# Key scaling moved to the head of each slot, own banks for the transposes, and every item of layer 1 by DMA

## The chip, the cores and the metric

One core of a Trainium2 chip runs the whole kernel. A core has five engines that each take their instructions in order: TensorE (PE, with its weight loads as PEld), VectorE (DVE), ScalarE (ACT), GpSimd (POOL) and SyncE (SP, which issues the DMAs here). They meet through semaphores only. The metric is the device time of one execution in microseconds, less is better.

## The reference

The model has two layers. Each adds a gated cross attention and a gated feed-forward to the residual x of 8 batches x 128 tokens x 512. What the change touches is the attention of layer 1 and the passage to its feed-forward:

```
q = (latents @ Wq), 32 heads of 128;  k, v = ([context, latents] @ Wk, Wv), 8 heads of 128
q = rms_norm(q, q_norm_w);  k = rms_norm(k, k_norm_w)
scores = einsum('bhgqd,bhkd->bhgqk', qg, k) * scale
probs  = softmax(scores);  out = einsum('bhgqk,bhkd->bhgqd', probs, v)
x = x + tanh(g_xattn[1]) * (out @ Wo)
x = x + tanh(g_ffn[1]) * (layernorm(x) @ weight.T + bias)
```

## The kernel before

Layer 1 is cut into 64 items: 8 heads of keys and values (the loop index t) times 8 batches (j). An item has 128 queries for each of four query heads and 256 keys, 128 from the context (computed in layer 0, loaded from HBM into kvc) and 128 from the latents. All products are made in three passes on a high and a low part of each operand, so nearly each tile has a "_hi" made by ScalarE and a "_lo" made by VectorE or POOL. What stands in the profile as fbias is, in this stage, k_sb (scaled keys) and k_sq (squares), which lie in that tensor; p is the probabilities, nb the shift of the exponentials, w_hi and w_lo the split weights of the next head.

The stage is a software pipeline written out by hand. Each engine has a function slot1(t, j), unrolled for t = 0 and t = 7 and looped for t = 1 to 6. In slot i (i = 8t+j) the engines work on several items at once, in this order:

- TensorE: keys_values(i+2) into the upper half of bank KVB; transposes of the queries of item i+1 into Q1B, and of its keys into the lower half of KVB; output_projection1(i-2) into Y1B; queries(i+2) into Q1B, which waits until qt_lo(i+1) has been read from there; the scores of item i+1 into S0B and S1B; attention_output1(i-1) into O1B.
- ScalarE: exponentials1(i), which waits for the shift nb; qt_hi and kt_hi of item i+1; pt_hi(i-1), the high part of the transposed probabilities (moved_probabilities_hi); kv_out(i+2), which copies the values and squares the keys of two tiles (the context's and TensorE's); q_out(i+2); output1_hi(i-1).
- VectorE: inverse sums of item i; qt_lo and kt_lo of item i+1; w_lo (split_lo) in slots 1 to 5 of each eight; accumulate1(i-2), drawn as "residual"; probabilities_in_blocks(i), two 32x32 block transposes; v_lo and k_ms of item i+2; w_hi (split_hi) in slots 0 to 4; k_scaled(i+2), which waits for POOL's root k_r; q_ss and q_ms; the maxima nmax and the shift nb of item i+1; output1_lo(i-1), ot_lo.
- POOL: normalises the probabilities of item i in two halves (p, L769); pt_lo(i-1) (L774); the roots k_r and q_r of item i+2 (L631).
- SyncE: the context's keys and values of item i+3; a piece of the next weights; then probabilities_round_trip(i): the blocks go out to DRAM, and four DMAs bring them back transposed.

The probabilities are transposed by that round trip for the first 60 items. For the last four (LAGGED = 60) TensorE transposes them into T0B and T1B, and ScalarE and VectorE split them from there. Behind the last slot stand the rest of the last items and the feed-forward: per batch, row statistics, normalised rows (plain), four transposes, a split, eight matmuls of 512 columns (last_ffn) and the addition to the residual; POOL adds the bias (L653).

## Time and profile before

| | |
|---|---|
| median of 3 runs | 1699.95 us (1699.6 to 1700.13) |
| profiled execution, its own time | 1700.84 us |
| its span | 1699.0 us |
| PE busy | 1651.3 us (97%) |
| DVE busy | 1216.1 us (72%) |
| ACT busy | 987.6 us (58%) |
| POOL busy | 771.7 us (45%) |
| DMA | 216.24 MB, mean 127 GB/s |

Busy time is the time in which an engine had an instruction drawn; a matmul's end is modelled, so PE's share hides small gaps. "<-" in brackets behind a row names what ended the wait in front of it. The span runs from the first to the last instruction; the rest of a run's time lies around it.

### The profile page before, as it was taken

How to read it: one execution, taken by the hardware profiler on the slowest of the kernel's cores; microseconds unless marked ns; L12 is line 12 of the kernel's file. 1: busy time of each engine (PE TensorE's matmuls, PEld its weight loads, DVE VectorE, ACT ScalarE, POOL GpSimd, SP SyncE). 2: the span in 40 equal slices, each digit the busy share in tenths (PEclk: the TensorE clock that was granted, in tenths of full speed). 3: DMA queues.
4: the chain of work that ended last, by engine and by line, in shares of the span. 5: the costliest groups of instructions: out<-in, count | busy, mean ns of one | idle time of the engine just before them, and what ended most of it. 6: DMA issues, size and time to landing. Idle time of an engine off the chain costs nothing.

```text
span 1699.0 us, 30580 instructions
## 1 busy us (share of the span) xinstructions
PE 1651.3 (97%) x9789; PEld 1426.0 (84%) x9789; DVE 1216.1 (72%) x2245; ACT 987.6 (58%) x2480; POOL 771.7 (45%) x644
## 2 busy tenths in 40 slices
PE   9999999999999999999999899999999999999998
PEld 8899999999988888888888777787878787777887
DVE  6444437676787777777788877777777777777777
ACT  5344343345767677676776566565656565665663
POOL 2422223211433443534435565566565656665554
PEclk9999999999999999999999999999999999999999
DMA  6444444545233333333332243434343444433311
GB/s 228 170 173 148 148 166 153 192 138 179 78 104 100 117 108 105 111 100 122 102 112 82 80 141 112 154 117 137 122 151 120 134 136 136 133 123 124 128 57 50
DMA packets 123792, 216.24 MB, mean 127 GB/s; under 512 B 11344, under 2 KB 93648, under 8 KB 120144
## 3 DMA queue, kind: packets, MB, share of 16 engines
q1 hardware_dynamic: 123728, 215.43, 38.0%
q8 instruction: 35, 0.57, 0.1%
q14 instruction: 29, 0.24, 0.0%
HBM read 139.89 MB, written 75.50 MB: 127 GB/s over the span
## 4 chain that ended last, share of the span: by engine, by line
PE 44%; DVE 28%; ACT 12%; issue 10%; POOL 4%; DMA 1%; DVEq 0%; SPq 0%; ACTq 0%; POOLq 0%
PE bank L2163 20%; ACT p L1237 7%; PE bank L2340 6%; DVE probabilities_in_blocks L1983 4%; PE bank L2110 4%; DVE v_lo L1922 3%; PE bank L2112 3%; PE bank L2111 3%; POOL k_r L631 3%; DVE nmax L1954 3%; DVE q_ss L1936 2%; PE bank L2298 2%; PE bank L2376 2%; DVE fbias L1929 2%; DVE qt_lo L2004 2%
## 5 line engine op out<-in xcount | busy, mean ns | idle before, releaser
L712 POOL TENSOR_TENSOR pr<-pr,rn 128x512 f32<-128x512 f32 x64 | 67.5, 1055 | 291.3 <-DVE rn L1610 291.3
L2110 PE MATMUL bank<-w_hi,xt_hi 128*128 (+2 forms) x512 | 182.5, 356 | 11.4 <-DVE qt_lo L2004 6.9
L769 POOL TENSOR_TENSOR p<-p,rn 128x512 f32<-128x512 f32 x128 | 133.2, 1041 | 128.3 <-DVE rn L1964 125.0
L1237 ACT ACTIVATE p<-bank,nb,q_r 128x256 f32<-128x256 f32 x256 | 141.2, 562 | 78.2 <-DVE nb L1959 78.1
L774 POOL TENSOR_TENSOR pt_lo<-probabilities_transposed,pt_hi 128x1024 fp32r<-128x1024 f32 x60 | 168.7, 2811 | 36.2 <-ACT pt_hi L1246 36.2
L2112 PE MATMUL bank<-w_hi,xt_lo 128*128 (+2 forms) x512 | 172.9, 338 | 0.0
L2111 PE MATMUL bank<-w_lo,xt_hi 128*128 (+2 forms) x512 | 172.2, 336 | 0.0
L2110 PEld LDWEIGHTS bank<-w_hi,xt_hi 128*128 128x128 f32 x512 | 96.3, 188 | 57.0 <-DVE qt_lo L2004 25.8
L2110 PE MATMUL bank<-w_hi,ot_hi 128*128 (+1 forms) x256 | 106.9, 418 | 18.3 <-DVE ot_lo L1992 16.1
L1079 ACT ACTIVATE pr<-sc,nmax 128x128 f32<-128x128 f32 x256 | 99.9, 391 | 39.8 <-DVE nmax L1595 39.4
L2110 PE MATMUL bank<-w0o_hi,ot_hi 128*128 128x512 f32 x256 | 105.4, 412 | 4.9 <-DVE residual L1602 4.4
L631 POOL TENSOR_TENSOR q_r<-q_ms,half 128x4 f32<-128x4 f32 x64 | 64.8, 1012 | 98.3 <-DVE q_ms L1938 98.3
L2112 PEld LDWEIGHTS bank<-w_hi,xt_lo 128*128 128x128 f32 x512 | 96.4, 188 | 11.1
L2163 PE MATMUL bank<-vw_hi,t_hi 128*128 128x256 f32 x368 | 104.1, 283 | 0.6 <-DVE vw_lo L1374 0.6
L2111 PEld LDWEIGHTS bank<-w_lo,xt_hi 128*128 128x128 f32 x512 | 96.7, 189 | 9.3
L2163 PE MATMUL bank<-vw_hi,t_lo 128*128 128x256 f32 x368 | 104.1, 283 | 0.0
L2163 PE MATMUL bank<-vw_lo,t_hi 128*128 128x256 f32 x368 | 104.1, 283 | 0.0
L2111 PE MATMUL bank<-w_lo,ot_hi 128*128 (+1 forms) x256 | 100.2, 391 | 0.0
L2112 PE MATMUL bank<-w_hi,ot_lo 128*128 (+1 forms) x256 | 100.2, 391 | 0.0
L2112 PE MATMUL bank<-w0o_hi,ot_lo 128*128 128x512 f32 x256 | 100.1, 391 | 0.0
L2111 PE MATMUL bank<-w0o_lo,ot_hi 128*128 128x512 f32 x256 | 100.0, 390 | 0.0
L1219 ACT ACTIVATE q_sb<-bank 128x512 f32<-128x512 f32 x64 | 38.3, 599 | 101.7 <-PE bank L2112 101.7
(298 smaller groups left out, 5517.8 us busy)
## 6 DMA issues: line engine op xcount, KB each, us to landing
blocks_of_probabilities<-probabilities_in_blocks SPq DMA_DIRECT2D x60, 512.0 KB, 2.9
probabilities_transposed<-blocks_of_probabilities SPq DMA_DIRECT2D x240, 128.0 KB, 2.8
stage<-w SPq DMA_DIRECT2D x35, 512.0 KB, 3.3
keys_of_layer<-kout SPq DMA_DIRECT2D x16, 1024.0 KB, 4.5
values_of_layer<-vout SPq DMA_DIRECT2D x16, 1024.0 KB, 5.2
kt<-keys_of_layer SPq DMA_DIRECT2D x64, 256.0 KB, 3.3
vs<-values_of_layer SPq DMA_DIRECT2D x64, 256.0 KB, 2.8
vraw<-wv SPq DMA_DIRECT2D x10, 1024.0 KB, 6.7
```

Source lines behind the costliest of these rows:

```text
L631: pool.tensor_tensor(dst, src, exponent, ALU.pow).then_inc(done, 1)
L712: pool.tensor_tensor(by4(pr), by4(pr), rn[:, :].unsqueeze(2).to_broadcast([P, 4, P]), ALU.mult).then_inc(norm_done, 1)
L769: pool.tensor_tensor(p1[:, half_p:half_p + 2, :], p1[:, half_p:half_p + 2, :], rn1[:, half_p:half_p + 2].unsqueeze(2).to_broadcast([P, 2, ...
L774: pool.tensor_tensor(pt_lo[:, :, :].rearrange("p kc (qb n) -> p kc qb n", qb=4), by_key_block(ptr1[:, (j - 1) % 2, :]), pt_hi[:, :, :].bit ...
L1079: last_op = nc.scalar.activation(by4(pr)[:, a, :], by4(sc)[:, a, :], ACT.Exp, bias=nmax[:, a:a + 1], accum_out=ssum[:, a:a + 1])
L1237: last_op = nc.scalar.activation(p1[:, a, :], by2((S0B, S1B)[a // 2][:, :])[:, a % 2, :], ACT.Exp, bias=nb1[:, a:a + 1], scale=q_r[:, pari ...
L1983: nc.vector.transpose(in_blocks(pblk[:, :])[:, half_p:half_p + 2], p1[:, half_p:half_p + 2, :].rearrange("p a (kc kb q) -> p a kc kb q", k ...
L2110: nc.tensor.matmul(out_ap, l_hi, r_hi, start=(c == 0), stop=False)
L2111: nc.tensor.matmul(out_ap, l_hi, r_lo, start=False, stop=False)
L2112: op = nc.tensor.matmul(out_ap, l_lo, r_hi, start=False, stop=(c == n - 1))
L2163: op = nc.tensor.matmul(out_ap, l, r, start=start, stop=False, skip_group_check=True)
L2340: op = nc.tensor.matmul(bank[which][:, :], l[:, a, c, :], r[:, c, :], start=start, stop=False, skip_group_check=True)
```

## The change

In layer 1's slots TensorE transposes keys and queries into banks of their own, KTB and QTB (which were T0B and T1B). keys_values no longer waits for kt_lo, queries waits for the copy and squares of the item before instead of for qt_lo, and the transposes wait for the qt_lo and kt_lo of the item before. ScalarE's kv_out(i+2) goes from the middle to the head of the slot, ahead of exponentials1(i). VectorE's k_mean(i+2) goes to the head of the slot, and v_low and k_scaled(i+2) right behind kt_lo, ahead of split_lo. POOL's k_root(i+2) goes to the head of the slot, ahead of the normalisation, while q_root(i+2) stays behind pt_lo. The special paths for the last four items go: all 64 take the round trip, with pt_hi and pt_lo on ScalarE and POOL. The order behind the last slot is written anew on all engines, and the banks of the last transposes and of the last feed-forward change. The rest of the diff takes out the special cases.

```diff
-        XT_BANK = ((6, 7) * 4, (0, 1, 4, 5, 0, 1, 4, 5), (4, 5, 6, 7) * 2, (0, 0, 1, 0, 1, 0, 1, 0))
+        XT_BANK = ((6, 7) * 4, (0, 1, 4, 5, 0, 1, 4, 5), (4, 5, 6, 7, 6, 7, 6, 7), (0, 1) * 4)
...
-        FFN_BANK = {1: (2, 3, 7, 2, 3, 7, 2, 3), 3: (1, 2, 3, 2, 3, 2, 3, 2)}
+        FFN_BANK = {1: (2, 3, 7, 2, 3, 7, 2, 3), 3: (4, 5) * 4}
...
-        KVB, Q1B, S0B, S1B, T0B, T1B, O1B, Y1B = bank
+        KVB, Q1B, S0B, S1B, KTB, QTB, O1B, Y1B = bank
...
@@ -759,35 +758,37 @@
+                if ahead:
+                    k_root(i + 2)
                 if not (first and j == 0):
+                    normalised(i)
+                if not (first and j < 2):
+                    probabilities_lo(i - 1, (j - 1) % 2)
+                if ahead:
+                    q_root(i + 2, (j + 1) % 2)
...
@@ -1203,12 +1209,12 @@
+                wait(act, k1_mean_done, count - 1)
...
-                        wait(act, kt1_lo_done, count - 1)
...
@@ -1246,44 +1249,33 @@
+                if not (last and j == BODY - 1):
+                    wait(act, o1_ps, i - 2)
+                    kv_out(i + 2, (j + 1) % 4, 4 * t + (j + 1) // 2 + 1)
                 if not (first and j == 0):
                     exponentials1(i, (j - 1) % 2)
...
-                if not (last and j == BODY - 1):
-                    wait(act, o1_ps, i - 2)
-                    kv_out(i + 2, (j + 1) % 4, 4 * t + (j + 1) // 2 + 1)
...
@@ -1311,12 +1299,14 @@
+            exponentials1(U, (BODY - 1) % 2)
             transposed_hi(3, 1)
-            exponentials1(U, (BODY - 1) % 2)
+            moved_probabilities_hi(U - 1, (U - 1) % 2)
             transposed_hi(3, 2)
             transposed_hi(3, 3)
-            probabilities_hi(U)
+            output1_hi(U - 1)
             transposed_hi(3, 4)
+            moved_probabilities_hi(U, U % 2)
             output1_hi(U)
...
@@ -1998,38 +1977,37 @@
+                if ahead:
+                    k_mean(i + 2)
                 if lag1:
                     inverse_sums1(i)
...
+                if ahead:
+                    v_low(i + 2, (j + 1) % 4)
+                    k_scaled(i + 2, (j + 1) % 4)
                 if not last and 1 <= j < 6:
                     split_lo(t + 1, j - 1, (t + 1) % 2)
...
-                if ahead:
-                    v_low(i + 2, (j + 1) % 4)
-                    k_mean(i + 2)
...
                 if ahead:
-                    k_scaled(i + 2, (j + 1) % 4)
                     q_mean(i + 2)
...
@@ -2518,7 +2490,6 @@
-                wait(pe, kt1_lo_done, count - 2)
                 wait(pe, k1_scaled, count - 1)
...
@@ -2527,7 +2498,8 @@
-                wait(pe, qt1_lo_done, count - 1)
+                wait(pe, q1_copied, count - 1)
+                wait(pe, q1_squared, count - 1)
...
@@ -2642,24 +2590,24 @@
+            output_projection1(U - 2, last_own)
+            last_ffn(1)
             transpose_rows(3, 2)
             transpose_rows(3, 3)
...
+            attention_output1(U - 1, (BODY - 2) % 4)
             last_ffn(2)
+            output_projection1(U - 1, last_own)
+            last_ffn(3)
             transpose_rows(3, 4)
             attention_output1(U, (BODY - 1) % 4)
-            last_ffn(3)
+            last_ffn(4)
             transpose_rows(3, 5)
-            output_projection1(U, (KV - 1) % 2)
+            output_projection1(U, last_own)
             transpose_rows(3, 6)
-            last_ffn(4)
             last_ffn(5)
+            last_ffn(6)
             transpose_rows(3, 7)
-            last_ffn(6)
             last_ffn(7)
```

## Rows read from the trace of the kernel before

**Rows 1.** one line in the source view: min/median/max ns, first and last start.
```profile
L2004 DVE TENSOR_TENSOR qt_lo<-bank,qt_hi x64: 678/692/694, 945.9 to 1664.1; 128x512 fp32r<-128x512 f32 x64
```

**Rows 2.** VectorE's timeline, a slot that splits weights: start us, us, instruction.
```profile
1253.15 0.69 DVE L2004 TENSOR_TENSOR qt_lo<-bank,qt_hi 128x512 fp32r<-128x512 f32 x1 [0.32 <-ACT qt_hi L1271]
1253.76 0.47 DVE L2006 SCALAR_TENSOR_TENSOR kt_lo<-bank,kw,kt_hi 128x256 fp32r<-128x256 f32 x1
1254.15 1.21 DVE L1912 TENSOR_TENSOR w_lo<-stage,w_hi 128x1024 f32 x1
1255.28 0.74 DVE L1968 SCALAR_TENSOR_TENSOR residual<-bank,tg,residual 128x512 f32<-128x512 f32 x1
1255.94 1.29 DVE L1983 STREAM_TRANSPOSE probabilities_in_blocks<-p 128x512 f32<-128x512 f32 x2
1257.16 0.62 DVE L1922 TENSOR_TENSOR v_lo<-keys_values_of_context,v_hi 128x128 fp32r<-128x128 f32 x1
1257.71 0.28 DVE L1922 TENSOR_TENSOR v_lo<-bank,v_hi 128x128 fp32r<-128x128 f32 x1
...
1257.97 0.68 DVE L1906 TENSOR_SCALAR w_hi<-stage 128x1024 f32 x1
1259.24 0.29 DVE L1929 TENSOR_SCALAR fbias<-keys_values_of_context,k_r 128x128 f32<-128x128 f32 x1 [0.59 <-POOL k_r L631]
...
1259.70 0.68 DVE L1936 TENSOR_REDUCE q_ss<-q_sq 128x4 f32<-128x512 f32 x1
...
1264.91 0.69 DVE L2004 TENSOR_TENSOR qt_lo<-bank,qt_hi 128x512 fp32r<-128x512 f32 x1 [0.32 <-ACT qt_hi L1271]
```

**Rows 3.** the timeline of VectorE around a slot without weights.
```profile
1298.75 0.69 DVE L2004 TENSOR_TENSOR qt_lo<-bank,qt_hi 128x512 fp32r<-128x512 f32 x1 [0.32 <-ACT qt_hi L1271]
...
1309.43 0.69 DVE L2004 TENSOR_TENSOR qt_lo<-bank,qt_hi 128x512 fp32r<-128x512 f32 x1 [0.33 <-ACT qt_hi L1271]
```

**Rows 4.** the timeline of TensorE's weight loads in the same slot.
```profile
1310.26 0.19 PEld L2110 LDWEIGHTS bank<-w_hi,xt_hi 128*128 128x128 f32 x1 [0.23 <-issue]
```

**Rows 5.** the timeline of ScalarE in the slot of rows 2.
```profile
1253.35 1.08 ACT L1246 ACTIVATE pt_hi<-probabilities_transposed 128x1024 fp32r<-128x1024 f32 x1
...
1254.79 0.29 ACT L1212 ACTIVATE v_hi<-bank 128x128 fp32r<-128x128 f32 x1
...
1262.10 0.56 ACT L1237 ACTIVATE p<-bank,nb,q_r 128x256 f32<-128x256 f32 x1 [1.70 <-DVE nb L1959]
```

**Rows 6.** the timeline of POOL in the slot of rows 2.
```profile
1254.50 3.13 POOL L774 TENSOR_TENSOR pt_lo<-probabilities_transposed,pt_hi 128x1024 fp32r<-128x1024 f32 x1 [0.56 <-ACT pt_hi L1246]
```

**Rows 7.** the timeline of POOL in the slot of rows 3.
```profile
1300.11 2.41 POOL L774 TENSOR_TENSOR pt_lo<-probabilities_transposed,pt_hi 128x1024 fp32r<-128x1024 f32 x1 [0.56 <-ACT pt_hi L1246]
```

**Rows 8.** the timeline of VectorE behind the last slot.
```profile
1678.19 1.04 DVE L1369 TENSOR_SCALAR plain<-residual,mv,roots 128x512 f32<-128x512 f32 x1
```

**Rows 9.** the timeline of POOL in the same microsecond.
```profile
1677.67 1.27 POOL L653 TENSOR_TENSOR residual<-residual,plain 128x512 f32<-128x512 f32 x1
```

**Rows 10.** the timeline of SyncE's DMA issues in the slot of rows 2.
```profile
1257.26 0.33 SPq L594 DMA_DIRECT2D blocks_of_probabilities<-probabilities_in_blocks  x1
1260.33 1.76 SPq L597 DMA_DIRECT2D probabilities_transposed<-blocks_of_probabilities  x4
```

**Rows 11.** part 6 of the page: DMA issues, KB each, median us to landing.
```profile
probabilities_transposed<-blocks_of_probabilities SPq DMA_DIRECT2D x240, 128.0 KB, 2.8
```

**Rows 12.** the timeline of TensorE: attention's first matmul and keys_values' last one.
```profile
1303.87 0.40 PE L2110 MATMUL bank<-pt_hi,v_hi 128*128 128x512 f32 x1
...
1306.55 0.28 PE L2112 MATMUL bank<-w_hi,xt_lo 128*128 x1
```

**Rows 13.** the timeline of VectorE in the last items and behind them.
```profile
1582.48 0.69 DVE L2004 TENSOR_TENSOR qt_lo<-bank,qt_hi 128x512 fp32r<-128x512 f32 x1 [0.32 <-ACT qt_hi L1271]
...
1687.48 0.75 DVE L1968 SCALAR_TENSOR_TENSOR residual<-bank,tg,residual 128x512 f32<-128x512 f32 x1 [1.19 <-PE bank L2112]
...
1695.72 0.75 DVE L1799 SCALAR_TENSOR_TENSOR residual<-bank,tg,residual 128x512 f32<-128x512 f32 x1 [1.09 <-PE bank L2460]
```

More of the change, by code:

```diff
@@ L612, in _ @@
                 slot1(KV - 1, j)
+            probabilities_round_trip(U, U % 4)
             for b in range(B):
@@ L1231, in exponentials1 @@
                 act.wait_ge(shift1_done, count)
-                if isinstance(count, int) and count > LAGGED + 1:
-                    act.wait_ge(pt1_ps, count - 1 - LAGGED)
-                else:
-                    wait(act, blocks1_done, 2 * (count - 1))
+                wait(act, blocks1_done, 2 * (count - 1))
                 for a in range(4):
@@ L1276, in slot1 @@
                     transposed_hi(2, 7)
[L1277 removed]
+                if not (first and j < 2):
                     moved_probabilities_hi(i - 1, (j - 1) % 2)
[L1279 to L1281 removed]
                 if first and j == 0:
@@ L1284, in slot1 @@
                     normed_rows(2, 7)
-                if not lagged(t, j) and i > LAGGED + 1:
-                    probabilities_hi(i)
                 if last and j == BODY - 1:
@@ L1293, in slot1 @@
                     transposed_hi(2, 5)
-                if (lagged(t, j) or i == LAGGED + 1) and not (first and j < 2):
+                if not (first and j < 2):
                     output1_hi(i - 1)
-                if not lagged(t, j):
-                    if i == LAGGED + 1:
-                        probabilities_hi(i)
-                    output1_hi(i)
                 if last and 3 <= j < 3 + C:
@@ L2059, in slot1 @@
                     split_hi(1, 0, 1)
-                if lagged(t, j) and not (first and j < 2):
+                if not (first and j < 2):
                     output1_lo(i - 1)
-                if not lagged(t, j):
-                    output1_lo(i)
             for j in range(BODY):
@@ L2595, in slot1 @@
                     pe.wait_ge(first_lo, 5)
-                if (lagged(t, j) or i == LAGGED + 1) and not (first and j < 3):
+                if not (first and j < 3):
                     output_projection1(i - 2, own if j >= 3 else other)
@@ L2612, in slot1 @@
                     pe.wait_ge(facc_done, B)
-                if not lagged(t, j) and i == LAGGED + 1:
-                    attention_output1(i - 1, (j - 2) % 4)
                 pe.wait_ge(qt1_lo_done, i + 1)
@@ L2621, in slot1 @@
                 op.then_inc(s1_ps, 1)
-                if lagged(t, j) and not (first and j < 2):
+                if not (first and j < 2):
                     if first and j == 2:
```

191 lines of the change are left out of this document (70 added, 121 removed).

## The prediction, made before the changed kernel was run

> **What bounds the kernel now.** I read the line view of the low query parts first [rows 1]. Each of the 64 items of layer 1 has one (qt_lo); they run from 945.9 to 1664.1 us, 11.40 us apart, so this stage is 42% of the span. Its neighbours on VectorE then give the real length of one slot: 11.76 us in a slot that splits weights (1253.15 to 1264.91) [rows 2], 10.68 us in one that doesn't [rows 3]. I write q for the start of qt_lo. TensorE's own work is nearly the short one: in it the weight loads stand still for only 0.23 us [rows 4], so a slot is about 10.45 us of TensorE. Five slots in eight are longer, and there the reader sees a ring of VectorE and ScalarE close on itself with hardly a gap, by starts [rows 2, 5]: qt_lo 0.61, kt_lo 0.39, w_lo 1.13, residual 0.66, blocks 1.22, v_lo with k_ms 0.81, w_hi 0.68, wait for k_r 0.59, k_scaled 0.46, and 5.21 from q_ss over maxima, shift and exponentials to the next qt_lo: 11.76. So VectorE's order sets these slots and TensorE the others. The page calls TensorE 97% busy, yet that hides the waits, since each matmul is drawn 0.40 long where the next starts 0.23 behind it.
>
> **Part 1: key work first.** On VectorE the wait of 0.59 for k_r goes (0.81 in the short slot), because POOL's root is now made while the exponentials run. k_mean moves into an idle gap: nothing. v_lo and k_scaled now stand right behind kt_lo: v_lo 0.40 (two of the 0.20 that the second takes, 1257.71 to 1257.91 by its 0.28 less the overlap), k_scaled 0.46 [rows 2]. The bare VectorE ring is 0.61+0.39+0.40+0.46+1.13+0.66+1.22+0.68+5.21 = 10.76 with weights to split, 10.76-1.13-0.68 = 8.95 without. If nothing else bound, slots would be 10.76 and 10.45, 5 us less in eight slots.
>
> **What the moves collide with.** POOL's pt_lo starts at q+1.35 (1254.50 against 1253.15) [rows 2, 6], and at q+1.36 in a short slot [rows 3, 7]. Today w_lo is ahead of it, from q+1.00, and pt_lo takes 3.13 instead of 2.41: it stands until w_lo is through [rows 2, 6, 7]. Later v_lo, from 1257.16, takes 0.62 and ends 0.15 behind pt_lo's end at 1257.63, while its twin takes 0.28 [rows 2, 6]. And a tensor_scalar of 0.54 or so that starts 0.52 into a POOL addition takes 1.04 and ends 0.28 behind it [rows 8, 9]. So whichever of the two engines starts first keeps the other out to its end, for VectorE reads of two SBUF tensors and for its SBUF-to-SBUF tensor_scalar. In the new order the first k_scaled starts at q+0.61+0.39+0.40 = q+1.40, and w_lo at q+1.86. If pt_lo starts at q+1.35, k_scaled comes 0.05 too late and stands to q+1.35+2.41 = q+3.76, less 0.25 that its front end already did: 2.1 us lost, straight in the ring. That gives 12.9 with weights and 11.05 without (11.75 in slot 0 of eight, which still has w_hi). The same holds for w_lo if pt_lo starts between q+1.40 and q+1.86. Behind q+1.86 nobody on VectorE waits, and pt_lo waits for w_lo instead.
> The Trainium skill has this as a rule against the change: "SBUF — State Buffer", Who interferes with whom, says that the shared port pair of VectorE and GpSimd is an exclusive lock, held by the first for its whole instruction. By that rule, the trace agrees: 3.13 against 2.41.
>
> **Part 2: squares before the exponentials.** ScalarE is in order. kv_out(i+2) now stands ahead of the exponentials of item i, and its second tile needs TensorE's keys_values(i+2), which stands behind attention_output(i-2), which needs pt_lo, which needs the transfers. Today the exponentials wait for the shift alone [rows 5]. That makes a second ring, over two slots: end of blocks to the last landing 3.1+1.3+2.8 = 7.2 (1260.33 less 1257.23, three quarters of the 1.76 that four issues take, and the median landing) [rows 10, 11], pt_hi to pt_lo 1.15 [rows 5, 6], pt_lo 2.41 [rows 7], attention and keys_values on TensorE 2.96 plus 0.1 of handing over [rows 12], second tile 0.45 (a read and a square like the 0.29 of it, overlapped) and exponentials to next qt_lo 2.81 [rows 5], from there to the end of blocks 0.61+0.39+0.40+0.46+1.13+0.66+1.29 = 4.94 [rows 2]. Sum 22.0, or 11.0 a slot; where pt_lo also waits for w_lo up to 1.13, 23.2 or 11.6. I take 11.6 for slots with w_lo, because pt_lo lands just there (below). The gain of part 1 is thus cut to 0.16 a slot, with no collision.
>
> **Where pt_lo falls.** In a free slot of 11.6 the landing is at q+4.94+7.2-11.6 = 0.55 into the next slot, pt_lo then at q+1.7: against w_lo, a collision. After a collided slot blocks end 2.1 later and the slot is 1.3 longer, so pt_lo starts at about q+2.5: no collision. So they alternate, as the landings scatter: two in the five slots with w_lo. Short slots have blocks at q+3.8, landing at q+0.55 of the next: k_scaled is just ahead by 0.3. One collision in three, I take that with w_hi. Eight slots: 5 x 11.6 + 3 x 10.45 = 89.4, plus 3 x 1.3 = 93.3. Today: (1582.48-945.9)/7 = 90.94 [rows 1, 13]. That is +2.3 or so for eight, over seven rounds +16.
>
> **Part 3: own banks.** TensorE's queries no longer wait for qt_lo (the 0.23 [rows 4], more in long slots) and keys_values not for kt_lo. Gain at most 0.23 in short slots; counted, in the 10.45. New waits (qt1_lo of the item before, squares of the item before) are a slot old: nothing. The ScalarE wait for kt_lo is gone, likewise nothing.
>
> **Part 4: all items by DMA, and the end.** TensorE loses four groups of eight transposes, VectorE gets block transposes for them. From qt_lo 57 (1582.48) to 64 are 81.6 us now [rows 1, 13]; the slots of this round split no weights. Seven at between 10.45 and 11.05, with row statistics and rows (2.5 us in all) on top: 77.5, or -4.1. Behind qt_lo 64, today 1695.72+0.75-1664.1 = 32.4 [rows 1, 13]. New chain: blocks of 63 end at q+2.9, transfers 7.2 to q+10.1; pt_hi, pt_lo 3.6 to 13.7; attention 1.6 to 15.3; ot_hi and ot_lo 1.9 with VectorE's queue to 17.2; output_projection 3.0 (twelve at 0.23 and 0.2) to 20.2; last_ffn(3) and rows(4) 2.5 to 22.7; pt_hi of item 64 stands behind transposed_hi(4) on ScalarE: 23.2; pt_hi, pt_lo 3.6 to 26.8; attention 1.6; ot 1.4; behind last_ffn(4) output_projection(64) ends at 33.4. From there today's end takes 1695.72+0.75-1687.48 = 9.0 [rows 13], the same then. 42.4, so +10.0. The transfers are exposed twice, which the PE transposes are not. Part 4 in all +6.
>
> **Sum** against the profiled run, 1700.84 (span 1699.0): +16 +6 = 1723; the profiled run stands 0.9 above the median 1699.95, so 1722. The ring bounds are rough and the short slots may be better than I take them: I say **1720**.
>
> **Rivals.** A, faster: pt_lo falls behind w_lo each time and no collision occurs. 89.4 for eight, -1.5 x 7 = -11, end +6, 1695; with the end also hidden 1689. For it: landings that scatter late push pt_lo behind q+1.86. Against: today's landings leave pt_hi free at once. B, collisions every other slot throughout: 5 slots with three, 3 with two: +5 x 1.3 = 95.9, +5 x 7 = +35, end +8: 1743. It decides as soon as landings take less than 7 us, because k_scaled is then late by 0.05 in short slots too. C, the forecast's mechanism with half the collisions: 89.4 + 1.5 x 1.3 = 91.3, +3, end +6: 1709. D, the exponentials never wait for keys_values, because TensorE runs ahead: slots of 10.76 and 10.45, four each, and three collisions of 2.1: 91.1, +1, end +6: 1707. E, gain and loss cancel: one collision in eight, where the slots with w_lo begin, 89.4 + 1.3 = 90.7, -2, and an end whose second transfer hides, +1: 1699.
>
> **How the numbers follow.** A measurement of this kernel can tell about 0.2%, 3.4 us. Forecast with B at its upper side 0.62 (forecast 0.5, B 0.12), C and D 0.2, E 0.08, A 0.10. Range: C, D, the forecast and the near half of E and of B, so 1698 to 1738; A and the far half of B stay out, some 0.2. Faster 0.10 (A), same 0.08 (E), slower 0.82.
>
> **What would show it.** Right: in the long slots a first k_scaled or w_lo of 2 us or more beside pt_lo; ScalarE's first exponential released by its own squares or by a PE bank, not by nb; pt_hi waiting for a DMA; slots of 11.6 and 12.9 in turn; no wait for k_r on VectorE; behind the last qt_lo some 42 us with TensorE idle before attention. Wrong: pt_lo always behind w_lo, slots of 10.8, or an end of 32 us. My prediction falls if VectorE isn't kept out by a POOL instruction that began only 0.05 earlier.

## The result and the profile after

The changed kernel takes 1762.85 us (median of 4 runs, 1755.27 to 1766.33) against 1700.03 us (1699.6 to 1700.13) on the same chip: ratio 1.0364, 95% interval 1.0342 to 1.0385. It is slower by 63 us, where 1720 and a range of 1698 to 1738 were predicted. The sign was right, the size was not: the time lies 25 us above the range.

The page of the changed kernel, its head and the parts that answer to the table of before:

```profile
span 1764.5 us, 30543 instructions
PE 1651.6 (94%) x9757; PEld 1448.0 (82%) x9757; DVE 1268.5 (72%) x2245; ACT 993.2 (56%) x2476; POOL 744.9 (42%) x648
```

TensorE's busy time is the same as before (1651.3), so by the page's count the 65.5 us by which the span grew are waiting. VectorE's busy time grew by 52.4 us though it gained hardly any work. The source view says where (one line of the kernel, min/median/max ns, first and last start):

```profile
L1919 DVE TENSOR_SCALAR fbias<-keys_values_of_context,k_r x64: 273/279/2452, 940.7 to 1707.2; 128x128 f32<-128x128 f32 x64
L1985 DVE TENSOR_TENSOR qt_lo<-bank,qt_hi x64: 679/692/694, 946.0 to 1717.6; 128x512 fp32r<-128x512 f32 x64
```

The first line is the first half of k_scaled: 0.28 us in most items, about 2.45 in 26 of the 64. One line got shorter: the first half of v_lo, which in the kernel before met the end of pt_lo in many slots, took 50.3 us for all 64 there and 18.7 here, so the change also takes a collision away. The second answers to [rows 1] and shows that the stage is now 771.6 us from first to last, 53.4 longer. Two slots of VectorE in its timeline, the first with the collision, the second without (start us, us, instruction, in brackets the idle time ahead and what ended it); they answer to [rows 2]:

```profile
1057.72 0.69 DVE L1985 TENSOR_TENSOR qt_lo<-bank,qt_hi 128x512 fp32r<-128x512 f32 x1 [0.32 <-ACT qt_hi L1268]
1058.33 0.47 DVE L1987 SCALAR_TENSOR_TENSOR kt_lo<-bank,kw,kt_hi 128x256 fp32r<-128x256 f32 x1
...
1059.12 2.45 DVE L1919 TENSOR_SCALAR fbias<-keys_values_of_context,k_r 128x128 f32<-128x128 f32 x1
1061.49 0.34 DVE L1919 TENSOR_SCALAR fbias<-bank,k_r 128x128 f32<-128x128 f32 x1
1061.75 1.21 DVE L1902 TENSOR_TENSOR w_lo<-stage,w_hi 128x1024 f32 x1
...
1067.44 0.16 DVE L1949 TENSOR_TENSOR nb<-nmax,q_r 128x4 f32<-128x4 f32 x1
1067.52 0.68 DVE L1971 TENSOR_TENSOR ot_lo<-bank,ot_hi 128x512 fp32r<-128x512 f32 x1
...
1070.53 0.69 DVE L1985 TENSOR_TENSOR qt_lo<-bank,qt_hi 128x512 fp32r<-128x512 f32 x1 [0.32 <-ACT qt_hi L1268]
...
1071.93 0.28 DVE L1919 TENSOR_SCALAR fbias<-keys_values_of_context,k_r 128x128 f32<-128x128 f32 x1
...
1073.52 0.75 DVE L1958 SCALAR_TENSOR_TENSOR residual<-bank,tg,residual 128x512 f32<-128x512 f32 x1
1074.18 1.29 DVE L1966 STREAM_TRANSPOSE probabilities_in_blocks<-p 128x512 f32<-128x512 f32 x2
1075.39 1.12 DVE L1896 TENSOR_SCALAR w_hi<-stage 128x1024 f32 x1
...
1078.89 0.16 DVE L1949 TENSOR_TENSOR nb<-nmax,q_r 128x4 f32<-128x4 f32 x1
...
1083.13 0.69 DVE L1985 TENSOR_TENSOR qt_lo<-bank,qt_hi 128x512 fp32r<-128x512 f32 x1 [0.32 <-ACT qt_hi L1268]
```

POOL's timeline in the same two slots (answers to [rows 6, 7]), then ScalarE's (answers to [rows 5]):

```profile
1059.08 2.41 POOL L770 TENSOR_TENSOR pt_lo<-probabilities_transposed,pt_hi 128x1024 fp32r<-128x1024 f32 x1 [0.56 <-ACT pt_hi L1249]
...
1073.55 2.42 POOL L770 TENSOR_TENSOR pt_lo<-probabilities_transposed,pt_hi 128x1024 fp32r<-128x1024 f32 x1 [2.22 <-ACT pt_hi L1249]
```

```profile
1057.89 1.10 ACT L1249 ACTIVATE pt_hi<-probabilities_transposed 128x1024 fp32r<-128x1024 f32 x1
...
1067.72 0.56 ACT L1240 ACTIVATE p<-bank,nb,q_r 128x256 f32<-128x256 f32 x1 [2.31 <-DVE nb L1949]
...
1072.41 1.06 ACT L1249 ACTIVATE pt_hi<-probabilities_transposed 128x1024 fp32r<-128x1024 f32 x1 [1.55 <-DMA probabilities_transposed<-blocks_of_probabilities]
...
1080.31 0.57 ACT L1240 ACTIVATE p<-bank,nb,q_r 128x256 f32<-128x256 f32 x1
```

Read the pair from the top. The first slot is slot 9 (slot i makes qt_lo of item i+1). In it pt_lo starts at q+1.36 and k_scaled 0.04 later: k_scaled stands to the end of pt_lo, 2.17 us too long, and the slot is 12.81. All VectorE work behind it is late by that, the block transposes too. So their transfers land late in the second slot: pt_hi waits 1.55 us for the DMA, pt_lo starts at q+3.02 instead of q+1.36, and now w_hi meets it (1.12 instead of 0.65). Attention, keys_values and kv_out follow late, and the exponentials start 1.42 us behind the start of nb, where 0.28 is usual, straight behind kv_out's squares: 12.60, of which 0.86 comes from the clock (below). Then it starts over. From slot 8 to slot 62 this comes strictly in turn: in every odd slot pt_lo starts between q+1.35 and q+1.70 and catches k_scaled (in three slots w_lo, which then takes 3.2 to 3.3 us); in every even one it starts at q+2.3 to q+3.8 and catches neither.

TensorE and ScalarE in all this: the view of waits between 1045 and 1580 us (us in total, times, longest), where [rows 4] showed 0.23 in a short slot.

```profile
PE bank L2080 <- DVE ot_lo L1971: 47.2, 21, 2.8
...
ACT pt_hi L1249 <- DMA probabilities_transposed<-blocks_of_probabilities: 37.6, 23, 2.4
ACT p L1240 <- DVE nb L1949: 36.4, 21, 2.3
...
PE bank L2080 <- POOL pt_lo L770: 8.1, 12, 1.4
```

There are 44 slots in that stretch. In 21 of them the exponentials waited for nb, in the other 23 they came straight behind kv_out. ot_lo, which stands behind nb on VectorE, is what TensorE waits for: 2.2 us on average, in about every second slot. The granted clock has a part in this, too. The view by stretches (us, busy us by engine, TensorE's clock, DMA share):

```profile
1069.10:1072.50 3.40, 3.40 (x10) 2.63 (x9) 2.15 (x9) 1.85 (x7) 2.08 (x2) 0.50 0.66 190
1072.50:1093.00 20.50, 18.40 (x110) 16.12 (x108) 17.23 (x31) 10.37 (x30) 9.63 (x7) 1.00 0.39 135
1093.00:1099.80 6.80, 6.13 (x14) 4.79 (x15) 4.69 (x13) 4.20 (x11) 3.79 (x4) 0.50 0.34 98
```

Just after the idle time of 2.8 us that ended at 1068.26 the clock is granted at 0.50, the lower of its two levels (1.2 GHz), for 3.4 us, and the matmuls of an output projection stand 0.43 apart instead of 0.23. The trace's record of the granted clock has 15 such stretches in layer 1 and behind it (two of them 6.8 us long); that of the kernel before has one.

What this costs can be read from the slots that split weights and follow a collided one (slots 2 and 4 of each eight). In the six middle rounds eight of these twelve had the clock at 0.50 at their start or just ahead of it, and took 12.44 to 13.82 us (12.87 on average). Four (slots 20, 34, 36 and 52) had it at 1.00 throughout and took 11.74, 11.93, 11.74 and 11.74 (11.79), though pt_lo started as late in them, at q+2.8 to q+3.1. TensorE's timeline, in slot 10 and then in slot 20 (qt_lo at 1195.73), shows the difference:

```profile
1070.31 0.63 PE L2080 MATMUL bank<-w_hi,ot_hi 128*128 x1
1070.74 0.63 PE L2081 MATMUL bank<-w_lo,ot_hi 128*128 x1
...
1076.88 0.40 PE L2080 MATMUL bank<-pt_hi,v_hi 128*128 128x512 f32 x1
...
1201.11 0.50 PE L2080 MATMUL bank<-pt_hi,v_hi 128*128 128x512 f32 x1 [0.42 <-POOL pt_lo L770]
```

In slot 20 attention starts at q+5.38, released by pt_lo. In slot 10 pt_lo ended at q+5.44, but attention starts at q+6.35 with no wait ahead of it: TensorE was still busy with the queries and scores that the half clock had held up. Eight slots times 1.08 are some 9 us in the six rounds, an estimate from these rows; in the short slots behind a collision the two kinds can't be told apart (12.2 to 12.6 either way).

Where the time went, by the first start of qt_lo of items 1, 9, 57 and 64 in VectorE's timeline of each kernel. "Eight" is a sixth of the way from 9 to 57.

| kernel | 1 | 9 | 57 | 64 | span | first eight | eight | 57 to 64 | behind 64 |
|---|---|---|---|---|---|---|---|---|---|
| before | 945.89 | 1036.61 | 1582.48 | 1664.13 | 1699.0 | 90.7 | 90.98 | 81.7 | 34.8 |
| changed | 946.05 | 1045.87 | 1635.49 | 1717.62 | 1764.5 | 99.8 | 98.27 | 82.1 | 46.9 |
| e4, banks alone | 945.44 | 1038.78 | 1584.80 | 1661.39 | 1710.3 | 93.3 | 91.00 | 76.6 | 48.9 |
| e1, pt_lo behind k_scaled | 946.01 | 1043.59 | 1593.22 | 1668.95 | 1715.7 | 97.6 | 91.61 | 75.7 | 46.7 |
| e2, behind w_lo too | 946.73 | 1043.72 | 1597.52 | 1673.37 | 1720.9 | 97.0 | 92.30 | 75.9 | 47.5 |
| e3, kv_out late | 944.63 | 1049.21 | 1635.83 | 1718.09 | 1767.3 | 104.6 | 97.77 | 82.3 | 49.2 |
| e12, e3 with e1's wait | 945.62 | 1042.30 | 1588.98 | 1665.46 | 1712.4 | 96.7 | 91.11 | 76.5 | 47.0 |
| e5, filler | 946.46 | 1046.17 | 1623.95 | 1709.25 | 1756.1 | 99.7 | 96.30 | 85.3 | 46.9 |
| e8, pt_lo in halves | 946.63 | 1044.28 | 1615.29 | 1693.31 | 1741.6 | 97.7 | 95.17 | 78.0 | 48.3 |
| e9, e1 and w_lo first | 946.28 | 1037.77 | 1558.39 | 1634.55 | 1682.5 | 91.5 | 86.77 | 76.2 | 47.9 |
| e11, e4, rows later | 946.14 | 1035.14 | 1581.69 | 1658.28 | 1705.7 | 89.0 | 91.09 | 76.6 | 47.4 |
| e6, before, w_lo first | 944.07 | 1033.34 | 1557.31 | 1639.15 | 1674.0 | 89.3 | 87.33 | 81.8 | 34.8 |
| e7, and k_mean first | 945.82 | 1032.35 | 1535.31 | 1615.91 | 1650.7 | 86.5 | 83.83 | 80.6 | 34.8 |
| e10, e4 with e7's moves | 946.03 | 1034.48 | 1536.54 | 1611.44 | 1660.2 | 88.5 | 83.68 | 74.9 | 48.8 |

So the 65.5 us are, rounded, 43.8 in the six middle rounds (7.29 each), 9.1 in the first round, 0.5 between items 57 and 64, 12.1 behind the last and 0.2 ahead of the first.

### The profile page after: what moved, and what is told of

Same layout as the page of the kernel before. It is cut to its first block, busy times and chain, and to the rows that moved or that the text cites. A ratio compares the mean times of both kernels' runs of the same rounds, so it can differ in the third digit from the quotient of the medians.

```text
span 1764.5 us, 30543 instructions
## 1 busy us (share of the span) xinstructions
PE 1651.6 (94%) x9757; PEld 1448.0 (82%) x9757; DVE 1268.5 (72%) x2245; ACT 993.2 (56%) x2476; POOL 744.9 (42%) x648
## 4 chain that ended last, share of the span: by engine, by line
PE 52%; DVE 21%; ACT 10%; DMA 7%; issue 5%; POOL 4%; SPq 1%; DVEq 0%; ACTq 0%; POOLq 0%
PE bank L2135 19%; PE bank L2080 7%; PE bank L2082 6%; PE bank L2081 6%; PE bank L2312 6%; DVE fbias L1919 4%; ACT p L1240 4%; DMA probabilities_transposed<-blocks_of_probabilities 3%; DMA blocks_of_probabilities<-probabilities_in_blocks 3%; POOL pt_lo L770 3%; DVE probabilities_in_blocks L1966 2%; PE bank L2270 2%; PE bank L2348 2%; DVE w_lo L1902 2%; PE bank L2432 2%
## 5 line engine op out<-in xcount | busy, mean ns | idle before, releaser
L770 POOL TENSOR_TENSOR pt_lo<-probabilities_transposed,pt_hi 128x1024 fp32r<-128x1024 f32 x64 | 154.8, 2419 | 96.1 <-ACT pt_hi L1249 96.1
L2080 PE MATMUL bank<-w_hi,ot_hi 128*128 (+1 forms) x256 | 115.0, 449 | 64.1 <-DVE ot_lo L1971 64.1
L2080 PE MATMUL bank<-w_hi,xt_hi 128*128 (+2 forms) x512 | 173.7, 339 | 0.1
L2080 PEld LDWEIGHTS bank<-w_hi,ot_hi 128*128 128x128 f32 x256 | 52.6, 206 | 81.0 <-DVE ot_lo L1971 62.5
L1255 ACT ACTIVATE ot_hi<-bank 128x512 fp32r<-128x512 f32 x64 | 38.3, 598 | 135.4 <-PE bank L2082 135.4
L2080 PEld LDWEIGHTS bank<-w_hi,xt_hi 128*128 128x128 f32 x512 | 97.0, 190 | 14.1 <-POOL w_lo L728 0.3
L2082 PE MATMUL bank<-w_hi,ot_lo 128*128 (+1 forms) x256 | 108.1, 422 | 0.0
L2081 PE MATMUL bank<-w_lo,ot_hi 128*128 (+1 forms) x256 | 107.6, 420 | 0.0
L2082 PEld LDWEIGHTS bank<-w_hi,xt_lo 128*128 128x128 f32 x512 | 96.8, 189 | 11.1
```

The lines of the kernel that those rows point to most:

```text
L770: pool.tensor_tensor(pt_lo[:, :, :].rearrange("p kc (qb n) -> p kc qb n", qb=4), by_key_block(ptr1[:, parity, :]), pt_hi[:, :, :].bitcast( ...
L2080: nc.tensor.matmul(out_ap, l_hi, r_hi, start=(c == 0), stop=False)
L2081: nc.tensor.matmul(out_ap, l_hi, r_lo, start=False, stop=False)
L2082: op = nc.tensor.matmul(out_ap, l_lo, r_hi, start=False, stop=(c == n - 1))
```

## The experiments

The theory after the result: the collision of pt_lo with k_scaled and w_lo makes nearly all of the loss, each time a whole one and in every second slot. Rivals: the exponentials' tie to keys_values (kv_out ahead of them), the granted clock, the transfers, the banks.

**e1, GpSimd waits for k_scaled.**

```diff
                 if not (first and j < 2):
+                    if ahead:
+                        pool.wait_ge(k1_scaled, i + 2)
                     probabilities_lo(i - 1, (j - 1) % 2)
```

> The changed kernel with one wait more on GpSimd: in each slot pt_lo starts only when VectorE's k_scaled of that slot is done. Nothing is left out of the computation. Collision theory: in the changed kernel 25 of 61 k_scaled took 2.2 us too long beside pt_lo (54.6 us in all); with the wait k_scaled is 0.28 us in every slot, pt_lo now falls beside w_lo (1.21 becomes up to 3.4 us) in some of the 35 slots that split weights, and the kernel comes to 1725 to 1745 us. Ring theory (the exponentials wait for kv_out, which waits for keys_values, attention and pt_lo): the slot stays at 12.3 us on average, since pt_lo is no earlier than before, and the kernel stays within 5 us of 1763. Clock theory (half-clock stretches make the time): as many stretches (15), no change.

Measured: 1715.84 us, ratio to before 1.0086 (1.0069 to 1.0103). One wait gives back 47 of the 63 us. The source view and the timelines of POOL and VectorE in a slot with weights:

```profile
L1921 DVE TENSOR_SCALAR fbias<-keys_values_of_context,k_r x64: 272/278/289, 940.6 to 1659.9; 128x128 f32<-128x128 f32 x64
```

```profile
1331.81 0.28 DVE L1921 TENSOR_SCALAR fbias<-keys_values_of_context,k_r 128x128 f32<-128x128 f32 x1
1332.01 0.34 DVE L1921 TENSOR_SCALAR fbias<-bank,k_r 128x128 f32<-128x128 f32 x1
1332.27 1.21 DVE L1904 TENSOR_TENSOR w_lo<-stage,w_hi 128x1024 f32 x1
```

```profile
1332.43 3.30 POOL L770 TENSOR_TENSOR pt_lo<-probabilities_transposed,pt_hi 128x1024 fp32r<-128x1024 f32 x1 [1.22 <-DVE fbias L1921]
```

No k_scaled is stretched. One expectation fell: w_lo isn't stretched either (1.21 in all 35), because it now starts 0.16 ahead of pt_lo, and pt_lo carries the delay (3.30 instead of 2.41). That costs less: attention starts straight behind pt_lo, at q+5.4, and the slot takes 11.7 where the collided one took 12.8. The run isn't free of collisions: w_hi still meets pt_lo's end in 33 of 35 slots (median 1.00 us). The clock came back with it: 4 stretches at 0.50 instead of 15.

**e2, GpSimd waits for w_lo too.**

```diff
                         pool.wait_ge(k1_scaled, i + 2)
+                    if not last and 1 <= j < 6:
+                        pool.wait_ge(w1_lo_done[j - 1], t + 1)
```

> As the run before, and in the five slots of eight that split weights pt_lo waits for w_lo too, so that it meets neither. Nothing is left out of the computation. Collision theory: VectorE loses only what is left beside w_hi (0.4 to 0.5 us where they meet), the slots come to 11.1 to 11.8 us and the kernel to 1705 to 1725 us. Ring theory: pt_lo ends up to 1.2 us later than in the run before, attention and keys_values with it, so the slots are longer: 1765 to 1780 us.

Measured: 1722.76 us, 1.0137 (1.012 to 1.0154), 7 more than e1. Neither number was met. The slots with weights are 11.9 to 12.0 instead of 11.7: no collision of k_scaled or w_lo was left to save, and pt_lo ends later, so that w_hi, which meets it in 33 of 35 slots in both runs, takes 1.26 us (median) instead of e1's 1.00. That is the 0.26 by which these slots grew. Of the two waits only the one for k_scaled brings anything.

**e8, pt_lo in two halves**, a dose of the collision.

```diff
-                pool.tensor_tensor(pt_lo[:, :, :]..., by_key_block(ptr1[:, parity, :]), pt_hi[:, :, :]..., ALU.subtract).then_inc(pt1_lo_done, 1)
+                for kc in range(2):
+                    last_op = pool.tensor_tensor(pt_lo[:, kc, :]..., by_key_block(ptr1[:, parity, :])[:, kc],
+                                                 pt_hi[:, kc, :]..., ALU.subtract)
+                last_op.then_inc(pt1_lo_done, 1)
```

> The changed kernel with GpSimd's pt_lo in two instructions of half the size (1.2 us each). Nothing is left out. Collision theory: a k_scaled that meets it waits for one half only, 0.3 to 1.2 us instead of 2.2, so the excess of k_scaled falls from 54.6 us to under 30, and the kernel by 15 to 30 us, to 1733 to 1748. Any other cause (transfers, clock, the tie of the exponentials): within 5 us of 1763.

Measured: 1743.31 us, 1.0259 (1.0242 to 1.0276), 20 us less than the changed kernel, as expected. VectorE's and POOL's timelines, of one collision:

```profile
1058.06 1.33 DVE L1922 TENSOR_SCALAR fbias<-keys_values_of_context,k_r 128x128 f32<-128x128 f32 x1
```

```profile
1058.02 2.55 POOL L771 TENSOR_TENSOR pt_lo<-probabilities_transposed,pt_hi 128x512 fp32r<-128x512 f32 x2 [0.56 <-ACT pt_hi L1252]
```

k_scaled stands for one half and gets in between the two. By the grouped line view the 64 first halves of k_scaled took 42.1 us together, in the changed kernel 74.2, with no collision 17.8 (e1): an excess of 24.3 instead of 56.4. In return w_lo is met more often: its 35 took 58.2 us instead of 50.6, with no collision 42.5. Both excesses together fall from 64.5 to 40.0, and the loss falls from 63 to 43. The loss falls with the time for which GpSimd keeps VectorE out.

**e3, the tie of the exponentials undone.**

```diff
-                if not (last and j == BODY - 1):
-                    wait(act, o1_ps, i - 2)
-                    kv_out(i + 2, (j + 1) % 4, 4 * t + (j + 1) // 2 + 1)
                 if not (first and j == 0):
                     exponentials1(i, (j - 1) % 2)
...
+                if not (last and j == BODY - 1):
+                    wait(act, o1_ps, i - 2)
+                    kv_out(i + 2, (j + 1) % 4, 4 * t + (j + 1) // 2 + 1)
                 if not (first and j < 2):
                     moved_probabilities_hi(i - 1, (j - 1) % 2)
```

VectorE's k_mean goes behind kt_lo and GpSimd's k_root behind the normalising with it.

> The changed kernel with ScalarE's kv_out behind the exponentials and the rounding of queries and keys (before the rounding of the probabilities), VectorE's k_mean behind kt_lo, GpSimd's k_root behind the normalising; v_low and k_scaled still ahead of w_lo, own banks, all items by DMA. Nothing is left out. Ring theory: the exponentials start 0.10 us behind nb in every slot, and the time falls by 20 to 45 us, to 1720 to 1745. Collision theory: k_scaled still falls beside pt_lo, at most 5 us less, 1758 to 1763, or more if it now waits for a later k_root.

Measured: 1768.75 us, 1.0416 (1.0393 to 1.0438): no gain, 6 us worse. The collisions move to w_lo (35 of them took 75.2 us together in the line view, in e1 42.5) and remain at k_scaled (46.8). The ring theory as the cause of the loss falls.

**e12, the tie undone and the collision too:** on top of e3

```diff
                 if not (first and j < 2):
+                    if ahead:
+                        pool.wait_ge(k1_scaled, i + 2)
                     probabilities_lo(i - 1, (j - 1) % 2)
```

> The changed kernel with kv_out and k_mean behind the exponentials (1768.8 us with the collisions) and now GpSimd's pt_lo waiting for k_scaled as well. Nothing is left out. It tells what the tie of the exponentials to keys_values costs once the collisions are gone: with kv_out ahead and the same wait the kernel took 1715.8, slots of 10.85 and 11.7. If the tie costs, the short slots fall to 10.4 to 10.6 and the kernel to 1700 to 1710. If the tie costs nothing, 1713 to 1718; if k_scaled, now a microsecond or two later, makes pt_lo late, 1725 to 1745.

Measured: 1714.99 us, 1.0095 (1.0077 to 1.0113), the same as e1. With the collision gone the place of kv_out and the key work that moves with it is worth nothing in sum: 91.11 us for eight against 91.61. By place in the round (medians), slot 5 fell from 11.7 to 11.2, slots 6 and 7 from 10.9 and 10.8 to 10.8 and 10.6, while slot 0 rose from 10.9 to 11.1 and slots 1 to 4 from 11.7 to 11.86. So the tie does cost something in the slots without w_lo, and what was moved to undo it costs as much elsewhere.

**e5, a filler on TensorE**, for the clock.

```diff
+                    wait(pe, acc1_done, i - 3)
+                    for n in range(8):
+                        nc.tensor.transpose(Y1B[:, tok(n % 4)], ident[:, :], ident[:, :])
                 if not (first and j < 3):
                     output_projection1(i - 2, own if j >= 3 else other)
```

> The changed kernel with eight idle transposes of the identity on TensorE ahead of each output projection of layer 1 (into that projection's own bank, which it then overwrites), about 1.2 us of TensorE a slot that fall into its wait for ot_lo (2.3 us on average). Nothing is left out. If half of the 63 us come from the granted clock of 0.5 (about 15 stretches of 3.4 us, some 1.5 us of matmuls lost in each), the stretches go and the time falls by 15 to 30 us, to 1735 to 1750. If the clock only follows from the waits and costs little, the stretches go and the time stays within 5 us of 1763, or rises by up to 10 where the filler outlasts the wait.

Measured: 1757.98 us, 1.0341 (1.0324 to 1.0359). The half-clock stretches between 1000 and 1670 us all went (mean clock of the span 0.994 against 0.984), and the time fell by 5 us. The six rounds that have the filler fell by 2.0 us each, 12 in all; between items 57 and 64, where it isn't, the time rose by 3. The run doesn't isolate the clock: it also has three collisions fewer (21 in slots 8 to 55 instead of 24), and a short collided slot grew from 11.08 to 11.26, which is the filler's own cost. Slot by slot it confirms what the rows of the changed kernel say: slots 10 and 18, 12.60 each there with the clock at 0.50, are 11.81 and 11.75 here, with pt_lo at q+2.99 and q+2.94. So the clock follows from the waits, and its own part is some 9 of the 63 us.

**e4, the banks and the DMA of all items alone**, with the key work of the three engines where it stood before. Against the changed kernel, VectorE's part (on ScalarE kv_out goes back behind pt_hi, on GpSimd k_root behind pt_lo):

```diff
-                if ahead:
-                    k_mean(i + 2)
...
-                if ahead:
-                    v_low(i + 2, (j + 1) % 4)
-                    k_scaled(i + 2, (j + 1) % 4)
...
                     probabilities_in_blocks(i)
...
+                if ahead:
+                    v_low(i + 2, (j + 1) % 4)
+                    k_mean(i + 2)
...
                     split_hi(t + 1, j, (t + 1) % 2)
                 if ahead:
+                    k_scaled(i + 2, (j + 1) % 4)
                     q_mean(i + 2)
```

> Own banks for the transposed keys and queries and all 64 items by DMA, but the key work of ScalarE, VectorE and GpSimd in the order of the kernel before. Nothing is left out. If the order of the key work is what costs: slots of 11.76 with weights and 10.45 to 10.7 without (90.0 to 90.9 us per eight), end as in the changed kernel (+12 us behind the last qt_lo, -4 for the seven slots), so 1700 to 1710 us. If the banks or the end cost more than I read: over 1715.

Measured: 1711.57 us, 1.0063 (1.0047 to 1.008). So of the 63 us the order of the key work makes 51 and the rest of the change 11.5. The rounds are those of before, 91.00 against 90.98: own banks bring nothing there. What costs is the first round (+2.6), and the end (57 to 64 gives back 5.1, behind 64 costs 14.1).

**e11, the rows behind the queries**, for the first slot.

```diff
-                if first and j < 2:
-                    transpose_rows(2, 4 + 2 * j)
-                    transpose_rows(2, 5 + 2 * j)
                 if ahead:
                     queries((j + 1) % B, other if j == BODY - 1 else own, i + 2)
+                if first and j < 2:
+                    transpose_rows(2, 4 + 2 * j)
+                    transpose_rows(2, 5 + 2 * j)
```

> The kernel with the banks alone (1711.6 us), and in the first two slots TensorE transposes the rows of layer 1 behind the queries and not ahead of them. Nothing is left out. With banks 4 and 5 given to keys and queries, the rows of item 4 go to bank 6, which is read until 948.2 of VectorE, and the queries stand behind them: TensorE is idle from 944.5 to 947.7. If that is the 3.6 us of the first slot, it falls from 13.7 to 10.2 to 10.8 us and the kernel to 1707 to 1709. If the wait only moves to another place, 1710 to 1713.

Measured: 1707.65 us, 1.0045 (1.0027 to 1.0063), 3.9 less than e4; the first slot is 9.32 us instead of 13.70. TensorE's timeline of the changed kernel at this place (in e4 the same wait is 3.19), then of e11:

```profile
944.73 0.38 PE L2553 MATMUL bank<-ident,fbias 128*128 128x128 f32 x2
949.21 1.68 PE L2104 MATMUL bank<-ident,z_mid 128*128 128x128 f32 x8 [4.10 <-DVE xt_lo L1349]
950.54 0.77 PE L2080 MATMUL bank<-w_hi,xt_hi 128*128 128x512 f32 x1
```

```profile
944.85 0.38 PE L2551 MATMUL bank<-ident,fbias 128*128 128x128 f32 x2
944.99 0.48 PE L2078 MATMUL bank<-w_hi,xt_hi 128*128 128x512 f32 x1
```

Keys and queries now own banks 4 and 5, so the rows of batches 4 and 5 go to 6 and 7, which VectorE's xt_lo still reads; the queries stood behind them for 4.1 us, in e4 for 3.2.

**e6 and e7, what bounds the kernel before.** The kernel before with w_lo at the head of VectorE's slot (e6), and with k_mean ahead of v_low as well (e7):

```diff
+                if not last and 1 <= j < 6:
+                    split_lo(t + 1, j - 1, (t + 1) % 2)
                 if lag1:
                     inverse_sums1(i)
...
-                if not last and 1 <= j < 6:
-                    split_lo(t + 1, j - 1, (t + 1) % 2)
...
-                    v_low(i + 2, (j + 1) % 4)
                     k_mean(i + 2)
+                    v_low(i + 2, (j + 1) % 4)
```

> The kernel before with one call moved: VectorE's w_lo of the five splitting slots stands at the head of the slot, where VectorE waits for the exponentials, and not behind kt_lo. Nothing is left out. If the loop nb - exponentials - qt_hi - kt_hi - kt_lo - VectorE's other work - nb is what gives 11.76 us (this is what I read in the trace of before), each splitting slot loses up to 1.2 us until pt_lo meets v_lo earlier: 87.4 us per eight instead of 91.0, the kernel at 1672 to 1682. If VectorE's order does not matter because the transfers or TensorE bound the slot, 1698 to 1702.

> As the run before, and k_mean stands ahead of v_low, so that v_lo's stretch beside pt_lo no longer holds up GpSimd's root of the keys. Nothing is left out. If that stretch stands on the path to k_scaled, TensorE's 10.44 us a slot become the bound: 84.0 to 85.0 us per eight, the kernel at 1652 to 1665. If not, the same as the run before within 3 us.

Measured: e6 1675.29 us, 0.9855 (0.9839 to 0.9872); e7 1653.01 us, 0.9717 (0.9701 to 0.9733). e7 is the fastest kernel here, 47 us below the kernel before and 110 below the changed one. VectorE's timeline of e7 in one slot with weights:

```profile
1221.83 0.69 DVE L2006 TENSOR_TENSOR qt_lo<-bank,qt_hi 128x512 fp32r<-128x512 f32 x1 [0.32 <-ACT qt_hi L1271]
...
1224.73 0.89 DVE L1917 TENSOR_SCALAR k_ms<-k_ss 128x2 f32<-128x2 f32 x1
1225.54 0.28 DVE L1922 TENSOR_TENSOR v_lo<-keys_values_of_context,v_hi 128x128 fp32r<-128x128 f32 x1
...
1229.27 0.16 DVE L1959 TENSOR_TENSOR nb<-nmax,q_r 128x4 f32<-128x4 f32 x1
1229.35 0.68 DVE L1992 TENSOR_TENSOR ot_lo<-bank,ot_hi 128x512 fp32r<-128x512 f32 x1
1229.95 1.21 DVE L1912 TENSOR_TENSOR w_lo<-stage,w_hi 128x1024 f32 x1
...
1232.37 0.69 DVE L2006 TENSOR_TENSOR qt_lo<-bank,qt_hi 128x512 fp32r<-128x512 f32 x1 [0.33 <-ACT qt_hi L1271]
```

w_lo lies in the time in which VectorE waited for the exponentials. That alone took the slot from 11.77 to 11.05 (e6), since v_lo now met pt_lo for longer (1.05 us on average). k_ms, two numbers a row, now meets pt_lo (0.89 instead of 0.15), but it is followed by v_lo and w_hi, while GpSimd makes the root; before, the root was only begun when the stretched v_lo was through. The slot is 10.54 (10.28 where no weights are split), and TensorE waits between 1045 and 1580 us for 8 us in all.

**e9, both cures in the changed kernel:** on top of e1

```diff
+                if not last and 1 <= j < 6:
+                    split_lo(t + 1, j - 1, (t + 1) % 2)
                 if ahead:
                     k_mean(i + 2)
...
-                if not last and 1 <= j < 6:
-                    split_lo(t + 1, j - 1, (t + 1) % 2)
```

> The changed kernel with both cures: GpSimd's pt_lo waits for k_scaled, and w_lo stands at the head of VectorE's slot. Nothing is left out. Against the changed kernel with the first cure alone (1715.8 us, slots of 11.7 with weights and 10.85 without): if its long slots are again VectorE's chain of which w_lo is a part, they fall to 10.9 to 11.1, 87.5 us per eight, 1690 to 1696. If they are the chain pt_lo - attention - keys_values - kv_out - exponentials - k_scaled - pt_lo, of which w_lo is no part but stretches pt_lo from 2.4 to 3.3, they fall to 10.85 to 10.9: nearly the same number. If neither, 1714 to 1718.

Measured: 1685.21 us, 0.9915 (0.9898 to 0.9933). Every slot is 10.8 to 10.9. **e10** is the kernel of e4 with e7's diff, word for word:

> Own banks and all 64 items by DMA with the order of the kernel before, and in it the two moves that brought the kernel before to 1653 us (w_lo at the head, k_mean ahead of v_low). Nothing is left out. If the own banks bring what I counted (0 to 0.23 a slot) the loop is at 82.0 to 83.8 us per eight against 83.8 there; the first slot and the end cost what they did in the kernel with the banks alone (3.6, and 14.1 less 5.1), so 1655 to 1666.

Measured: 1659.9 us, 0.9761 (0.9744 to 0.9779). Its rounds are e7's, 83.68 against 83.83, so even at TensorE's own pace the banks bring 0.15 us in eight slots, and with the first slot and the end it is 6.9 us behind e7. The weight loads' waits between 1045 and 1580 us, one line from e9 and one from e7:

```profile
PEld bank L2082 <- POOL pt_lo L770: 19.4, 49, 0.7
```

```profile
PEld bank L2110 <- DVE qt_lo L2006: 7.6, 29, 0.3
```

With the keys' scaling ahead of pt_lo, TensorE still waits for pt_lo in each of 49 slots, 0.4 us at a time, and 0.4 is what a slot of e9 (10.85) has over one of e7. So with w_lo out of the ring in both, the changed order is a little ahead of the old one in the rounds (86.77 us for eight in e9, 87.33 in e6); it loses to the old order with k_mean ahead of v_low (83.83 in e7, 83.68 in e10), and over the whole kernel to e6 as well, by its first slot and its end.

## Why the prediction was wrong in size

**What bounds the kernel before:** right for the long slots. The ring of VectorE and ScalarE was read as 11.76 with w_lo in it. Taking w_lo out gave 11.05, and k_mean ahead of v_low 10.54 (e6, e7). For the short slots TensorE was named as the bound, with 10.45 of work. That was wrong: moving k_mean on VectorE alone took them from 10.68 (e6) to 10.28 (e7), so VectorE's order held these too, through v_lo beside pt_lo and the late root.

**Part 1, the collision:** right in kind, place and size. Predicted was pt_lo at q+1.35, k_scaled at q+1.40, 2.1 us lost, a slot of 12.9; measured 1.36, 1.40, 2.17 and 12.81. The prediction said that it would fall if VectorE weren't kept out by an instruction that began only 0.05 earlier; 0.04 was enough. One collision was missed: w_hi in the slots behind. This is also the rule that it cited from the Trainium skill ("SBUF — State Buffer", Who interferes with whom): the trace agrees with it, 2.45 us with pt_lo whole and 1.33 with pt_lo in halves.

**Where pt_lo falls:** this is the step that failed first, in its count. The prediction said that collided and free slots alternate and then counted only two in the five slots with w_lo and one in the three short ones, on the ground that landings scatter and that k_scaled would be 0.3 ahead in the short slots. The alternation was strict: four collisions in eight slots, the short slot 7 among them. The scatter doesn't break it. In 24 of the 27 collided slots from slot 9 on the transfers had landed early, so pt_lo started right behind ScalarE's exponentials, qt_hi, kt_hi and pt_hi, at q+1.36, 0.04 ahead of k_scaled. In the other three (slots 21, 35 and 37) pt_hi waited for the landing, to q+0.38 to q+0.57, and pt_lo started at q+1.52 to q+1.70: that is the forecast's own case (q+0.55 and q+1.7), and it catches w_lo instead. Both cases collide. That is rival B's pattern (a collision in every other slot throughout), which had a chance of 0.12 and a time of 1743.

**The price of one** was taken as 1.3, with the slot behind it at its free length. With the clock at 1.00 that is about right. Against e1 (medians by place in the round) a collided slot and the one behind it are longer by 1.3 (slots 1 and 2), 1.1 (3 and 4), 1.9 (5 and 6) and 1.3 us (7 and 0), 1.4 on average. Slots 1 and 3 pay it themselves, and slots 2 and 4 then have e1's length (11.74) in spite of the late landing; of slots 5 and 7 most is carried over by the late landing into 6 and 0. What was missing is **the clock**, which was no term of the sum: TensorE's waits for ot_lo brought 15 stretches at 0.50, some 9 us in the six rounds, 1.4 in each.

**The rounds without a collision** were put at 89.4 and are 91.61 in e1, whose added wait is part of its own ring (91.2 by medians, as one slot took 14.05); the short slots are 10.8 to 10.9, not 10.45. Whether the changed order without any added wait would reach 89.4 can't be seen: no run had it free of collisions.

For eight slots 93.3 was forecast and 98.27 measured. The 5.0 between them are, roughly, one collision more (1.3), the price (0.4), the clock (1.4) and the base (1.8).

**Part 2, the tie:** it is there, as foretold (in 23 of 44 slots the exponentials were not released by nb, and pt_hi waited for a DMA 23 times), but it isn't what makes the loss: e3 and e12 undo it, with k_mean and k_root moved along, and gain nothing in sum. It is how a short slot behind a collision takes over the delay.

**Part 3, own banks:** a gain of at most 0.23 in short slots was counted; measured nothing in the rounds (91.00 against 90.98, and 83.68 against 83.83). What was missed is their price: the banks of the transposed rows changed with them, and the first slot became 13.70 in e4 and 14.93 in the changed kernel instead of 10.07. That line of the diff was shown and not costed. e11 gives 3.9 us of it back.

**Part 4, the end:** nearly right where no collision disturbs it: +6 was forecast for the last round and the end together, and e1 has +6.0, the changed kernel +12.6. From the last qt_lo to the last residual 42.4 was predicted, 10.0 more than before. VectorE's timeline of the changed kernel at the last item (its qt_lo starts at 1717.62), then POOL's, which answer to [rows 13]:

```profile
1752.64 0.75 DVE L1958 SCALAR_TENSOR_TENSOR residual<-bank,tg,residual 128x512 f32<-128x512 f32 x1 [0.98 <-PE bank L2082]
...
1761.29 0.75 DVE L1789 SCALAR_TENSOR_TENSOR residual<-bank,tg,residual 128x512 f32<-128x512 f32 x1 [1.54 <-PE bank L2432]
```

```profile
1741.93 2.34 POOL L770 TENSOR_TENSOR pt_lo<-probabilities_transposed,pt_hi 128x1024 fp32r<-128x1024 f32 x1 [3.69 <-ACT pt_hi L1249]
```

1761.29+0.75-1717.62 = 44.4. The last pt_lo ends 26.7 behind qt_lo (26.8 predicted) and the last output projection's residual starts at 35.0 (33.4). Here the clock was at 0.50 once, for 3.4 us from 1744.9. The 4.1 us between items 57 and 64 came true only where there was no collision: -5.1 in e4, -5.9 in e1, +0.5 in the changed kernel.

Together, against the kernel before: the collisions, with the clock that falls behind them, +49 (1764.5 less e1's 1715.7) where 27 were counted; everything else +17 (e1, 1715.7 less 1699.0), of it in e1 +5.8 in the first slot, +12 behind the last, -5.9 between items 57 and 64 and +4 in the six rounds, where the prediction had -5 in all.

## What to carry to other kernels

When a VectorE instruction with two SBUF inputs, or an SBUF-to-SBUF tensor_scalar, is moved, lay its new start beside the starts of GpSimd's instructions: if both follow from the same event their distance is fixed, and a collision then happens every time or never, not now and then. Cost it with the slot behind it and with TensorE's clock, which falls when TensorE is made to wait, and try the wait that puts GpSimd second: it was one line and gave back 47 us. And before moving the work at the end of a ring, look for the gap in which its engine waits: w_lo moved there, and a two-number k_ms moved ahead of a stretched v_lo, made the kernel 47 us faster with none of the change's parts.
